# Relative attention's DRAM scratch cut from 64 heads to 16, each place written and read four times

## The chip, the cores and the metric

The kernel runs on one core of one Trainium2 chip. The metric is the device time of that core, from the launch of the program to its end, in microseconds (us). One execution was also taken by the hardware profiler; its rows are what the prediction is made from.

## What is computed

The input x has 4 sequences of 512 positions and 128 features. The program first adds a relative attention of 16 heads with 8 features each, and then six layers of windowed attention and a gated feed-forward. The change touches the first part alone. Cut to what matters:

```
x = x + attn(layernorm(x))          # the part that is changed
x = x + ffn(layernorm(x))           # six layers of local attention and feed-forward

# attn: B = 4 sequences, S = 512, H = 16 heads, P = 8 features of a head
pos = sinusoid_pos_emb(S, D) @ Wp + bp
content_score = einsum('bhsp,bhtp->bhst', q + u, k)
pos_score     = einsum('bhsp,htp->bhst', q + v, pos)
pos_score     = relative_shift(pos_score)
weights = softmax((content_score + pos_score) / sqrt(P))
out = einsum('bhst,bhtp->bhsp', weights, val)   # then @ Wo + bo

def relative_shift(x):              # per head: pad one column, reread with rows one shorter
    x = pad(x, one zero column on the left)     # [S, S + 1]
    return x.reshape(S + 1, S)[1:, :]           # [S, S]
```

All data is float32. There are 4 x 16 = 64 heads, each with a 512 x 512 matrix of position scores.

## The kernel before

The relative shift needs a row to be reread under another row length, which the kernel does through DRAM. The position scores of a head are written to `scratch_w` as 512 rows of 513 values (one zero column ahead), and read back as 512 rows of 512 values from one row further on. `scratch_w` has 64 heads, so each is written once and read once, at a place of its own.

The work goes in 128 rounds `r` (`ROUNDS`). A round handles a pair of heads and one of the four steps `i` of 128 rows; two rounds make one transfer `n = r // 2`, so a pair of heads takes two transfers (`n // 2` is the number of the pair), and there are 64 writes and 64 reads. Each queue and engine runs its own program in order:

- TensorE makes the position scores of round r (L905, `ps_b<-posm,qvT`), and 20 rounds behind (`LAG`) the content scores of round c = r - 20 (L905, `ps_b<-kTm,quT`), the transposes of round c - 1 (L931), and the sums with the values (L950).
- ScalarE (ACT) copies the position scores of round r to `wrows` (L1004), a ring of `NW` = 4 transfers. Before it fills a slot again it waits until the write that used it has landed (`written`). 12 rounds behind (`READ_AT`) it issues the read of transfer n into `shifted` (L1013), a ring of `NR` = 6, after a wait for the two writes of that pair and for VectorE to have taken the slot's last contents. It also does the exponentials (L1020).
- The SyncE queue (SP) issues the write of transfer n (L896) once the four copies of it are done (`w_copied`). It has nothing else to do in this stage.
- VectorE (L967) waits at round c for the read of transfer c // 2 (`read`), adds it to the content scores and takes the row's extreme into `lowest`; GpSimd (POOL, L991) scales the result `less`.

A write takes two heads' 128 partitions with two steps' rows each, 1026 KB in packets of 4104 bytes; a read is 1024 KB in packets of 4096 bytes. All transfers of the stage run on the same 16 DMA engines. The stage ends with a barrier of all engines before the output projection (L1037 and on), and the six layers follow.

Of the kernel before, what the change touches and what calls it, by code (L numbers as in the profile page):

```python
# [5 lines left out]
F32, BF16, I32 = mybir.dt.float32, mybir.dt.bfloat16, mybir.dt.int32  # L6
# [4 lines left out]
BATCH, SEQ = 4, 512  # L11
# [5 lines left out]
H0, DP = 16, 8  # L17
# [21 lines left out]
def at_least(eng, sem, count):  # L39

    if count > 0:
        eng.wait_ge(sem, count)
# [682 lines left out]
def relative_attention(nc, x, w, scratch):  # L725
# [7 lines left out]
    with ExitStack() as ctx:  # L733
# [3 lines left out]
        def sem(name):  # L737
            return ctx.enter_context(nc.semaphore("a_" + name))

        S = SEQ  # L740
        STEPS = S // P
# [12 lines left out]
        with ExitStack() as first:  # L754
# [16 lines left out]
            with nc.Block() as block:  # L771
                @block.sync
                def _(sp):
                    for dst, src in ((ident[:, :], w["ident"]), (wpT[:, :], w["wpT"][:, :, 0, :].rearrange("h p d -> (h p) d")),
                                     (table[:, :], w["fcols"][:, 1, 0:S]), (wproj[:, :, :], w["wproj"]),
                                     (cols[:, :], w["cols"]), (rows[:, :, :], w["rows"])):
                        sp.dma_start(dst, src).then_inc(s["loaded"], 16)
# [77 lines left out]
        with ExitStack() as second:  # L855
            def sb2(name, shape):
                return second.enter_context(nc.sbuf_tensor(name, shape, F32))
# [5 lines left out]
            ROUNDS = UNITS * STEPS * 2  # L863
            LAG, READ_AT = 20, 12
            NW, NR = 4, 6
            wrows = sb2("wrows", [P, NW, 2, 2, S + 1])
            shifted = sb2("shifted", [P, NR, 2, 2, S])
            less = sb2("less", [P, 2, 2, S])
# [9 lines left out]
            read = [sem(f"read{n}") for n in range(NR)]  # L878
            flat = scratch.rearrange("n s c -> n (s c)")

            def of(r):

                return r // (2 * STEPS), r % STEPS, r // STEPS % 2 * 2

            def in_slot(slots, n):
                return 16 * (n // len(slots) + 1)

            with nc.Block() as block:
                @block.sync
                def _(sp):  # L890

                    for n in range(ROUNDS // 2):
                        u, i, g = of(2 * n)
                        sp.wait_ge(s["w_copied"], 4 * n + 4)
                        rows_of = scratch[4 * u + g:4 * u + g + 2, :, :].rearrange("h (p i) c -> p h i c", i=STEPS)
                        sp.dma_start(rows_of[:, :, i:i + 2, :].rearrange("p h i c -> p h (i c)"),  # L896
                                     wrows[:, n % NW, :, :, :].rearrange("p h i c -> p h (i c)")).then_inc(written[n % NW], 16)

# [95 lines left out]
                @block.scalar  # L994
                def _(act):
                    act.wait_ge(s["zeroed"], 1)
                    for r in range(ROUNDS + LAG + 6):
                        c = r - LAG
                        if r < ROUNDS:
                            n = r // 2  # L1000
                            at_least(act, written[n % NW], 16 * (n // NW))
                            for k in range(2):
                                act.wait_ge(s["w_made"], 2 * r + k + 1)
                                nc.scalar.copy(wrows[:, n % NW, k, r % 2, 1:S + 1], ps[:, k, :]).then_inc(s["w_copied"], 1)  # L1004
                        n = (r - READ_AT) // 2
                        if r % 2 == 0 and 0 <= n < ROUNDS // 2:

                            u, i, g = of(2 * n)
                            for done in range(n // 2 * 2, n // 2 * 2 + 2):
                                act.wait_ge(written[done % NW], in_slot(written, done))  # L1010
                            at_least(act, s["c_taken"], 4 * (n - NR + 1))
                            src = flat[4 * u + g:4 * u + g + 2, S:(S + 1) * S].rearrange("h (p i t) -> p h i t", i=STEPS, t=S)
                            act.dma_start(shifted[:, n % NR, :, :, :].rearrange("p h i t -> p h (i t)"),  # L1013
                                          src[:, :, i:i + 2, :].rearrange("p h i t -> p h (i t)")).then_inc(read[n % NR], 16)
                        t = c - 1
                        if 0 <= t < ROUNDS:
                            at_least(act, s["o_summed"], t // 2 - 1)
                            for k in range(2):
                                act.wait_ge(s["p_turned"], 2 * t + k + 1)
                                nc.scalar.activation(pT[:, t // 2 % 2, t % 2 * 2 + k, :], ps[:, 4 + k, :], ACT.Exp  # L1020
                                                     ).then_inc(s["p_ready"], 1)
                        m = (c - 3) // 2
                        if c % 2 and 0 <= m < UNITS * STEPS and m % STEPS == STEPS - 1:
                            n = m // STEPS
                            act.wait_ge(s["o_summed"], m + 1)
                            at_least(act, s["o_turned"], n)
                            nc.scalar.copy(oT[:, :], ps[:, 6, :]).then_inc(s["o_copied"], 1)
# [36 lines left out]
def whole_kernel(nc, x_in, out, attention, layers):  # L1064
    with ExitStack() as ctx:
        x1 = ctx.enter_context(nc.sbuf_tensor("x1", [P, TILES, D], F32))
        x_loaded, added, stored = (ctx.enter_context(nc.semaphore(n)) for n in ("x_loaded", "x_added", "out_stored"))
        scratch = nc.dram_tensor("scratch_w", [BATCH * H0, SEQ, SEQ + 1], F32).ap()
        tiled = "(t p) d -> p t d"
        with nc.Block() as block:  # L1070
            @block.sync
            def _(sp):
                sp.dma_start(x1[:, :, :], x_in.rearrange("b s d -> (b s) d").rearrange(tiled, p=P)).then_inc(x_loaded, 16)
                sp.wait_ge(x_loaded, 16)
        relative_attention(nc, x1, attention, scratch)
        x = ctx.enter_context(nc.sbuf_tensor("x", [P, TILES, D], F32))
        layer_norm_tiles(nc, x1, x, "norm2")
        local_layers(nc, x, layers)
        with nc.Block() as block:
            @block.vector  # L1080
            def _(dve):
                nc.vector.tensor_tensor(x[:, :, :], x[:, :, :], x1[:, :, :], ALU.add).then_inc(added, 1)  # L1082

            @block.sync
            def _(sp):
                sp.wait_ge(added, 1)
                sp.dma_start(out.rearrange("b s d -> (b s) d").rearrange(tiled, p=P), x[:, :, :]).then_inc(stored, 16)
                sp.wait_ge(stored, 16)
# [88 lines left out]
```

## Time and profile before

| what | value |
|---|---|
| device time, median of 3 runs | 2430.02 us (2418.19 to 2435.28) |
| device time of the profiled execution | 2422.32 us |
| its span (first to last instruction) | 2420.5 us |
| TensorE busy / VectorE / ScalarE / GpSimd | 87% / 63% / 50% / 58% of the span |
| DMA, whole program | 260.54 MB, mean 108 GB/s |
| mean granted TensorE clock | 0.959 of full speed |

The span is one execution; what lies around it is 2422.32 - 2420.5 = 1.8 us. The busy shares are means over stages that differ: the relative attention fills about the first fifth of the span, the six layers the rest. In the rows, "SPq" and "ACTq" are DMA issues of those engines' queues, "to landing" is the time from the issue of a transfer to its last signal, and a DMA share of 1.00 means that on average all 16 DMA engines had a packet under way (it passes 1.00 where packets of the two queues overlap on one engine).

### The profile page before, as it was taken

To read this page: it belongs to the slowest core of one execution; us is meant where nothing else is said; L and a number is where in the kernel's file an instruction comes from. 1 tells how busy PE (TensorE), PEld (TensorE's weight loads), DVE (VectorE), ACT (ScalarE), POOL (GpSimd) and SP (SyncE) were. 2 spreads that over 40 slices of the span, in tenths; PEclk is the share of its full clock that TensorE was granted. 3 is DMA by queue.
4 is the path that set the end of the run, shared out by engine and by line. 5 is a ranking of instruction groups with operands and counts; after the bars stand their busy time and mean duration, and the time that the engine had idled before them with its cause. 6 is when DMAs were issued, how large, how long until landed. Compare 5 with 4: busy or idle time off the path is not lost. (4 is left out here: it accounts for less than half of the span.)

```text
span 2420.5 us, 84613 instructions
## 1 busy us (share of the span) xinstructions
PE 2096.9 (87%) x36003; PEld 1418.7 (59%) x36003; DVE 1529.2 (63%) x2264; ACT 1217.4 (50%) x1652; POOL 1395.7 (58%) x2272
## 2 busy tenths in 40 slices
PE   4687788893889899999999999898999999999996
PEld 2154445552666666666666666666666666666664
DVE  4043334443777677777777767777777777777773
ACT  2365556741445555544555445554455445555542
POOL 0043334444776676676666666666666666676770
PEclk9599989996999999999999999999999999999998
DMA  1799999942222322232222322223222242222221
GB/s 48 221 310 283 270 293 318 366 153 59 72 62 63 97 60 58 63 94 61 65 57 59 97 61 66 55 57 104 57 64 57 57 109 61 55 67 58 57 63 28
DMA packets 124948, 260.54 MB, mean 108 GB/s; under 512 B 29300, under 2 KB 40224, under 8 KB 123808
## 3 DMA queue, kind: packets, MB, share of 16 engines
q1 hardware_dynamic: 107168, 188.03, 29.0%
q10 hardware_dynamic: 17408, 67.11, 9.6%
q8 instruction: 287, 4.70, 0.9%
q14 instruction: 85, 0.70, 0.1%
HBM read 86.08 MB, written 68.29 MB: 64 GB/s over the span
## 5 line engine op out<-in xcount | busy, mean ns | idle before, releaser
L223 POOL TENSOR_TENSOR roped<-turned 128x512 f32<-128x512 f32 x384 | 480.4, 1273 | 386.4 <-PE ring L424 381.9
L414 PE MATMUL ring<-wqkv,xT 128*128 128x512 f32 x1152 | 573.0, 620 | 6.0 <-ACT squares L288 4.0
L568 DVE TENSOR_TENSOR turned<-ring,ropes 128x1024 f32<-128x1024 f32 x384 | 451.4, 1217 | 99.8 <-PE ring L414 97.8
L991 POOL TENSOR_SCALAR less<-less,lowest 128x512 f32<-128x512 f32 x256 | 174.4, 692 | 347.8 <-DVE lowest L967 347.8
L258 POOL TENSOR_TENSOR roped<-roped,rnorm 128x1024 f32<-128x1024 f32 x192 | 361.1, 1902 | 13.8
L967 DVE CUSTOM_DVE_ANT_0 less<-ps_b,shifted 128x512 f32<-128x512 f32 x256 | 166.7, 689 | 311.6 <-PE ps_b L905 190.7
L414 PEld LDWEIGHTS ring<-wqkv,xT 128*128 128x128 f32 x1152 | 198.7, 192 | 173.2 <-issue 153.9
L347 ACT COPY oT<-ring 128x1024 f32<-128x1024 f32 x96 | 97.2, 1012 | 364.8 <-PE ring L476 364.8
L577 DVE TENSOR_REDUCE ss<-squares 128x16 f32<-128x1024 f32 x192 | 232.9, 1213 | 37.5 <-ACT squares L288 37.5
L905 PE MATMUL ps_b<-posm,qvT 32*128 32x512 f32 x512 | 171.0, 744 | 95.6 <-ACT wrows L1004 72.1
L1004 ACT COPY wrows<-ps_b 128x512 f32<-128x512 f32 x256 | 137.5, 590 | 192.4 <-PE ps_b L905 118.0
L288 ACT ACTIVATE squares<-ring 128x1024 f32<-128x1024 f32 x192 | 197.2, 1027 | 60.1 <-DVE turned L568 59.6
L613 DVE TENSOR_TENSOR attended<-ring,rinv 128x1024 f32<-128x1024 f32 x96 | 117.6, 1225 | 170.0 <-PE ring L466 170.0
L485 PEld LDWEIGHTS yps<-wo,oT 128*128 128x128 f32 x1536 | 187.9, 193 | 47.1 <-issue 45.6
L424 PE MATMUL ring<-ident_l,roped 128*128 128x128 f32 x1536 | 193.5, 277 | 15.0 <-POOL roped L258 14.7
L466 PEld LDWEIGHTS ring<-vwin,pT 64*32 64x32 f32 x12288 | 129.6, 105 | 120.1 <-ACT pT L340 60.2
L424 PEld LDWEIGHTS ring<-ident_l,roped 128*128 128x128 f32 x1536 | 175.3, 143 | 32.1 <-POOL roped L258 19.1
L485 PE MATMUL yps<-wo,oT 128*128 128x128 f32 x1536 | 188.9, 276 | 2.0 <-ACT oT L347 1.1
L466 PE MATMUL ring<-vwin,pT 64*32 64x64 f32 x12288 | 148.6, 226 | 44.0 <-issue 27.6
L334 ACT ACTIVATE probs<-probs 128x1024 f32<-128x1024 f32 x96 | 101.6, 1059 | 156.1 <-DVE probs L591 156.1
L931 PEld LDWEIGHTS ps_b<-ident_a,less 128*128 128x128 f32 x1024 | 115.9, 146 | 101.5 <-POOL less L991 63.0
L441 PEld LDWEIGHTS ring<-kT,qT 64*32 64x32 f32 x12288 | 138.6, 105 | 60.2 <-issue 57.3
(122 smaller groups left out, 3383.4 us busy)
## 6 DMA issues: line engine op xcount, KB each, us to landing
vwin<-v SPq DMA_DIRECT2D x1536, 64.0 KB, 2.3
scratch_w<-wrows SPq DMA_DIRECT2D x64, 1026.0 KB, 21.7
shifted<-scratch_w ACTq DMA_DIRECT2D x64, 1024.0 KB, 20.6
wqkv<-in_l_wqkv SPq DMA_DIRECT2D x6, 1536.0 KB
wo<-in_l_wo SPq DMA_DIRECT2D x24, 128.0 KB
w<-in_l_w SPq DMA_DIRECT2D x6, 342.0 KB
w<-in_l_w SPq DMA_DIRECT2D x6, 171.0 KB
out_dram<-x SPq DMA_DIRECT2D x1, 1024.0 KB, 5.1
```

The lines of the kernel that those rows point to most:

```text
L223: nc.gpsimd.tensor_tensor(halves[2][:, :, side, :], halves[0][:, :, side, :], halves[1][:, :, 1 - side, :], ALU.add).then_inc(s[name + "_a ...
L258: nc.gpsimd.tensor_tensor(whole, whole, norm, ALU.mult).then_inc(s[name + "_roped"], 1)
L288: nc.scalar.activation(squares[:, n, :], ring[:, room(name.upper()), :, :].rearrange("p b c -> p (b c)"), ACT.Square).then_inc(s[name + "_ ...
L414: last = nc.tensor.matmul(out[:, half, :], xT[:, t % SEQT * P:(t % SEQT + 1) * P], wqkv[:, layer_of(t), at + half * 512:at + (half + 1) * ...
L424: last = nc.tensor.transpose(out[:, j * P:(j + 1) * P], roped[:, n, j * P:(j + 1) * P], ident[:, :])
L466: last = nc.tensor.matmul(out[W * win:W * win + W, r, j * DH:(j + 1) * DH], pT[rows, j, W * win:W * win + W], vwin[rows, p, win, j * DH:(j ...
L485: last = nc.tensor.matmul(out[:, 0:D], oT[:, j, :], wo[:, layer_of(t), j, :], start=j == 0, stop=j == PAIRS - 1)
L568: ins = nc.vector.tensor_tensor(turned[:, n, part, :].rearrange("p (h d) -> p h d", d=DH), heads, table, ALU.mult)
L577: nc.vector.tensor_reduce(ss[:, n * HEADS:(n + 1) * HEADS], squares[:, n, :].rearrange("p (h d) -> p h d", d=DH), AX.X, ALU.add).then_inc( ...
L905: nc.tensor.matmul(ps[:, bank + k, :], q[at, here:here + P], keys(at, u % VARS, b), start=True, stop=True).then_inc(signal, 1)
L967: nc.vector.tensor_tensor_reduce(less[:, c % 2, k, :], ps[:, 2 + k, :], shifted[:, c // 2 % NR, k, c % 2, :], -SCALE0, HIGHEST, ALU.add, A ...
L991: nc.gpsimd.tensor_scalar(less[:, c % 2, k, :], less[:, c % 2, k, :], -1.0, lowest[:, c % 2, k:k + 1], ALU.mult, ALU.add).then_inc(s["scal ...
```

## The change

`scratch_w` is declared with 16 heads instead of 64. The pair with number `n // 2` uses place `(n // 2) % 8` of it, for its two writes and its two reads. From transfer 16 on, SP waits before each write until both reads of the pair that had the place before, transfers `(n // 2 - 8) * 2` and the next one, have landed. Nothing else differs: the instructions of every engine and their order are the same, the sizes and shapes of the transfers too.

```diff
             NW, NR = 4, 6
+            KEPT = scratch.shape[0] // 2
...
+            def place(pair):
+                return pair % KEPT * 2
...
                     for n in range(ROUNDS // 2):
                         u, i, g = of(2 * n)
                         sp.wait_ge(s["w_copied"], 4 * n + 4)
-                        rows_of = scratch[4 * u + g:4 * u + g + 2, :, :].rearrange("h (p i) c -> p h i c", i=STEPS)
+                        if n // 2 >= KEPT:
+
+                            for done in range((n // 2 - KEPT) * 2, (n // 2 - KEPT) * 2 + 2):
+                                sp.wait_ge(read[done % NR], in_slot(read, done))
+                        rows_of = scratch[place(n // 2):place(n // 2) + 2, :, :].rearrange("h (p i) c -> p h i c", i=STEPS)
                         sp.dma_start(rows_of[:, :, i:i + 2, :].rearrange("p h i c -> p h (i c)"),
                                      wrows[:, n % NW, :, :, :].rearrange("p h i c -> p h (i c)")).then_inc(written[n % NW], 16)
...
-                            src = flat[4 * u + g:4 * u + g + 2, S:(S + 1) * S].rearrange("h (p i t) -> p h i t", i=STEPS, t=S)
+                            src = flat[place(n // 2):place(n // 2) + 2, S:(S + 1) * S].rearrange("h (p i t) -> p h i t", i=STEPS, t=S)
...
-        scratch = nc.dram_tensor("scratch_w", [BATCH * H0, SEQ, SEQ + 1], F32).ap()
+        scratch = nc.dram_tensor("scratch_w", [H0, SEQ, SEQ + 1], F32).ap()
```

## Rows read from the trace of the kernel before

**Rows 1.** Windows: busy us (count) by engine, granted clock, DMA share, GB/s.

```profile
54.70:115.90 61.20, 39.45 (x80) 9.53 (x80) 0.01 (x1) 19.46 (x38) 0.00 (x0) 0.50 0.68 208
115.90:180.00 64.10, 55.42 (x616) 33.03 (x616) 28.53 (x89) 41.43 (x80) 27.57 (x41) 0.94 1.08 311
180.00:400.00 220.00, 171.41 (x1892) 102.35 (x1892) 80.53 (x255) 127.08 (x243) 80.10 (x118) 0.92 1.05 287
...
410.00:490.00 80.00, 70.49 (x847) 42.80 (x848) 37.03 (x118) 56.45 (x109) 36.43 (x54) 1.00 1.03 365
490.00:545.60 55.60, 51.38 (x564) 31.12 (x560) 26.13 (x82) 21.92 (x41) 26.23 (x39) 1.00 0.39 125
545.60:2420.50 1874.90, 1678.10 (x31814) 1182.28 (x31812) 1327.40 (x1619) 930.97 (x1110) 1215.46 (x2008) 0.98 0.26 66
```

**Rows 2.** Waits from 200 to 400 us: total us, times, longest.

```profile
DVE less L967 <- PE ps_b L905: 65.6, 26, 4.9
ACT wrows L1004 <- DMA scratch_w<-wrows: 58.6, 21, 4.1
...
PEld ps_b L905 <- ACT wrows L1004: 49.6, 27, 3.5
```

**Rows 3.** Waits from 410 to 485 us.

```profile
ACT wrows L1004 <- DMA scratch_w<-wrows: 4.3, 3, 2.3
```

**Rows 4.** Transfers of scratch_w issued from 180 to 400 us.

```profile
L1013 ACTq DMA_DIRECT2D shifted<-scratch_w x30: 366/366/367, 180.9 to 397.9; - x30
L896 SPq DMA_DIRECT2D scratch_w<-wrows x29: 359/359/360, 185.2 to 394.8; - x29
...
DMA to landing us min/median/max: 19.6/25.3/30.0
```

**Rows 5.** Transfers of scratch_w issued from 410 to 490 us.

```profile
L896 SPq DMA_DIRECT2D scratch_w<-wrows x13: 359/360/363, 414.3 to 485.7; - x13
...
DMA to landing us min/median/max: 11.6/16.5/20.0
```

**Rows 6.** Transfer 16's write, the first that would reuse a place.

```profile
L896 SPq DMA_DIRECT2D scratch_w<-wrows x1: 360/360/360, 155.6 to 155.6; - x1
```

**Rows 7.** Transfer 1's read, the later of the two it would wait for.

```profile
L1013 ACTq DMA_DIRECT2D shifted<-scratch_w x1: 367/367/367, 96.2 to 96.2; - x1
...
DMA to landing us min/median/max: 9.4/9.4/9.4
```

**Rows 8.** The closest pair: write of transfer 62.

```profile
L896 SPq DMA_DIRECT2D scratch_w<-wrows x1: 363/363/363, 479.8 to 479.8; - x1
```

**Rows 9.** And the read of transfer 47, for which it would wait.

```profile
L1013 ACTq DMA_DIRECT2D shifted<-scratch_w x1: 367/367/367, 423.1 to 423.1; - x1
...
DMA to landing us min/median/max: 18.5/18.5/18.5
```

**Rows 10.** Timeline around an ACT read issue, which has three waits.

```profile
89.48 0.59 ACT L1004 COPY wrows<-ps_b 128x512 f32<-128x512 f32 x1 [2.21 <-PE ps_b L905]
89.59 0.39 ACTq L1013 DMA_DIRECT2D shifted<-scratch_w  x1
```

**Rows 11.** DMA issues of the page: size, median us to landing.

```profile
scratch_w<-wrows SPq DMA_DIRECT2D x64, 1026.0 KB, 21.7
shifted<-scratch_w ACTq DMA_DIRECT2D x64, 1024.0 KB, 20.6
```

**Rows 12.** Windows of 10 us each, columns as in rows 1.

```profile
80.00:90.00 10.00, 6.22 (x12) 1.50 (x12) 0.00 (x0) 3.36 (x8) 0.00 (x0) 0.50 0.45 180
90.00:100.00 10.00, 6.22 (x12) 1.50 (x12) 0.00 (x0) 3.36 (x8) 0.00 (x0) 0.50 1.03 234
100.00:110.00 10.00, 6.23 (x12) 1.50 (x12) 0.00 (x0) 3.36 (x7) 0.00 (x0) 0.50 1.02 228
110.00:120.00 10.00, 6.82 (x23) 2.20 (x24) 1.84 (x5) 2.95 (x7) 1.37 (x2) 0.50 1.00 359
240.00:250.00 10.00, 7.26 (x78) 4.27 (x80) 3.36 (x13) 5.12 (x10) 3.71 (x6) 0.83 1.10 245
...
280.00:290.00 10.00, 9.38 (x118) 5.83 (x116) 4.12 (x13) 6.47 (x13) 4.19 (x7) 0.96 1.06 325
```

## The prediction

> **What bounds the kernel now.** I read the windows first, since the change touches one stage. The reader should see in [rows 1] that the relative attention's exchange with DRAM runs from 54.7 to about 545.6 us, and that its bound changes on the way. From 180 to 400 us the DMA engines are full (share 1.05) and yet move only 287 GB/s, while no engine is busy for more than 171.4 of 220 us (TensorE) and its granted clock is down at 0.92. From 410 to 490 us they are as full (1.03) but move 365 GB/s, and TensorE is busy for 70.5 of 80 us at clock 1.00. The same transfers, so, are slow in one stretch and fast in another.
>
> The list of waits says the same from the engines' side. In the slow stretch ScalarE stands for 58.6 us, 21 times, before it may fill a slot of `wrows` whose write hasn't landed, and TensorE's weight loads for 49.6 us on ScalarE's copies [rows 2]. VectorE's largest wait (65.6 us) is for TensorE's scores, which is the same delay handed on: its own wait for a read hardly shows. In the fast stretch ScalarE's wait for writes is 4.3 us [rows 3]. Thus the chain in the slow stretch is write landing, copy, scores, next write; in the fast one it is the round's compute.
>
> The pace per transfer comes from the issues. 29 writes from 185.2 to 394.8 us are 28 steps, 209.6 / 28 = 7.49 us each [rows 4]; 13 writes from 414.3 to 485.7 us are 12 steps, 71.4 / 12 = 5.95 us each [rows 5]. One step moves a write and a read, 1026 + 1024 KB [rows 11], 2.10 MB. 2.10 MB in 7.49 us is 280 GB/s and in 5.95 us 353 GB/s, near what [rows 1] has for these stretches. What follows at 545.6 us, 1874.9 us of layers, comes after a barrier and isn't touched by the change, so each us won or lost here is one at the end.
>
> **Part 1, the new waits.** 48 writes (transfers 16 to 63) each get two waits on reads. The question is whether such a read can still be out. Transfer 16 is written at 155.6 us [rows 6]; it would wait for reads 0 and 1, and read 1 is issued at 96.2 us and lands 9.4 us later, at 105.6 [rows 7]. That leaves 50.0 us. I went through all 48 pairs by their issue times: the closest is write 62 at 479.8 us [rows 8] with read 47, issued at 423.1 us and landed at 441.6 [rows 9], 38.2 us ahead. Even with the longest landing of the slow stretch, 30.0 us [rows 4], it would be 56.7 - 30.0 = 26.7 us ahead. The code says that this is no luck of one execution: the copies of transfer n need TensorE's round 2n, and TensorE gets there only after the transposes of round 2n - 22, thus after VectorE has taken round 2n - 22, whose read (transfer n - 11) has then landed. The wait asks for transfers n - 16 and n - 15 at most. The wait can't be the last to be met whatever the rates are. Its stall is 0.
>
> What is left is the time of the instructions themselves on SP's sequencer. No row has SP with three waits. From below it is 0, and a gain is excluded, for a wait that is met takes no work away. From above, the nearest row is ScalarE's queue: a read's issue, which has two waits for writes and one for VectorE ahead of it, stands 0.11 us after the start of the copy before it [rows 10]. With 0.11 us on each of 48 writes and all of it on the path, that is 5.3 us. I take 0, because the write then meets a DMA queue that is full: it lands 19.6 us or more after its issue in the slow stretch [rows 4] and 11.6 us or more in the fast one [rows 5], so several transfers are in flight and the engines have other packets to work on. In the fast stretch ScalarE needs the landing only three steps later. If that cover were gone the 5.3 us would be the price. Queued behind the waiting instruction is SP's next write and nothing else, for SP has no other work in this stage; who waits for it would be ScalarE (slot of `wrows`, and its read's issue).
>
> **Part 2, the addresses.** This is what the change really changes: the number of bytes, packets and transfers stays, the order stays, the distance between a write and its read stays, but 64 heads' worth of DRAM becomes 16. What this does to the rate of a transfer no row shows, as every place is used once. So it is bounded from both sides over the 47 steps from write 16 (155.6 us, [rows 6]) to write 63 (485.7 us, [rows 5]), 330.1 us, or 7.02 us a step.
> - Gain at most: all 47 steps at the fast stretch's pace, which TensorE then sets: 47 x 5.95 = 279.7 us, 50.4 us less.
> - Loss: the slow stretch's pace for all, 47 x 7.49 = 352.0 us, 21.9 us more. Further out, the lowest rate with reads and writes side by side is 228 GB/s [rows 12], 2.10 / 0.228 = 9.2 us a step, 432 us, 102 us more.
>
> Which is nearest? The first 16 heads have been seen: while transfers 10 to 17 are written and 5 to 13 are read, the stretch of 115.9 to 180 us moves 311 GB/s at share 1.08 [rows 1], 6.75 us a step. And they show both a 228 and a 359 GB/s within 20 us [rows 12], as do the heads of the middle (245 and 325 within 40 us, [rows 12]). If the rate hung on the place alone, the 16 heads kept would run at 311 GB/s: 47 x 6.75 = 317 us, 13 us less than now. If it hangs on how the two queues' packets meet in time, nothing changes. Rates that swing this much within one place speak for the second; I take 0, and keep 13 us of gain as part of the range of this case.
>
> The same row of 287 GB/s at a full share [rows 1] can be held against a rule. The Trainium skill (DMA: Bandwidth & Descriptors, section Latency and other measured facts) reports that DMA copies with row pitches of large powers of two lose half of their rate or more, that a few KiB of padding restores it, and that this doesn't depend on how many tiles are touched; it calls the mechanism an inference. Here the head's pitch (513 x 512 x 4 bytes, 1 MiB and 2 KiB) and the row's pitch are the same before and after, and only the number of places falls, so by that rule the term is 0 too, where a reading of the rows by place gives 13 us less. No row here tests it.
>
> **Sum.** 2422.3 us (the profiled execution) + 0 (stall) + 0 (issue) + 0 (rate) = 2422.3 us. That execution is 7.7 us under the median of the three runs, 2430.0 us, which range over 17 us. The best guess of a new median is between the two: 2426 us. About 1% (24 us) is what a measurement of this kernel can tell from no change.
>
> **The rivals.**
> - *The smaller region is easier on DRAM.* The slow stretch goes away in part or in whole. For it: something slows the middle that doesn't slow heads 50 and on, and heads 0 to 15 are at the faster side (311 against 287 GB/s). Against it: the swings inside any group of heads. In whole it gives 2426 - 50 = 2376 us; half of it 2401 us. It counts as faster by over 1% from 24 us on, when the mean step falls below 7.02 - 24 / 47 = 6.51 us, 323 GB/s.
> - *Writes and reads now run over the same 16 heads and hinder each other (slower).* Before, each write went to a place never touched; now a write of place p comes while other places of the same 16 MB are read, and a write follows a read of the same bytes. For it: with writes alone the engines move 180 GB/s at a share of 0.45, and as soon as reads join, at 90 us, only 234 at 1.03 [rows 12], so the two kinds do disturb each other. Against it: they do that at distinct places already, and a read still follows its write by 6 transfers. It decides from 24 us on: a mean step above 7.53 us, below 279 GB/s. At the slow stretch's pace throughout it would be 2448 us, still within 1%; at 245 GB/s [rows 12], 8.6 us a step, 2426 + 73 = 2499 us; at 228, 2528 us.
> - *The new wait bites.* It needs a read that lands more than 56.7 us after its issue [rows 8, 9], against at most 30.0 [rows 4], and the code's order excludes it. Its cost would be a stall of the only write queue, but I see no case for it.
> - *The change doesn't do what it says*, for instance because places were already reused. In the code they weren't, with 64 heads and no modulus.
>
> **How the numbers follow.** No change beyond noise, with the small gain of 13 us and the 5.3 us loss inside: 0.60. The first rival by over 1%: 0.24, since there is a clear slow stretch to win back and the place is one of two explanations for it. The second by over 1%: 0.15. A wait or anything else that costs over 1%: 0.01. So faster 0.24, same 0.60, slower 0.16. The range that should hold 8 in 10 leaves out the first rival near its full size (below 2385 us, 0.09) and the second at its worst (above 2470 us, 0.09). The likeliest case's own range is 2405 to 2445 us: the runs' own 2418 to 2435, less 13 us and more some 10 us for a slow stretch that reaches further.
>
> **What the profile of the changed kernel would show.** If right: 64 writes and 64 reads of the same sizes; no wait of SP for reads, and SP's issues right behind the copies; a first stage that again ends near 545 us, with a slow stretch whose rate is 260 to 330 GB/s at a share over 1, ScalarE's wait for writes about 60 us in it and a granted clock of about 0.92. The slow stretch needn't lie at the same time. If the first rival is right, ScalarE's wait for writes falls to a few us, the clock stays at 1.00 from 120 us on, 360 GB/s hold to the end of the writes, and the stage ends near 495 us. If the second is right, the rate drops from transfer 16 on, at about 156 us, and not before. The prediction fails if the rate of a DRAM transfer depends on the region that it goes to by more than 8%.

## The result, and the profile after

The changed kernel takes 2416.23 us (median of 20 runs, 2408.74 to 2422.51), the kernel before 2426.68 us (median of 20 runs, 2416.53 to 2437.08). The ratio is 0.9956 with a 95% interval of 0.9943 to 0.997: 10.5 us less, within 1%, but clear of the noise. The forecast was 2426 us and no change. In the third group of experiments below, one of the nine executions of the kernel before took 7783.93 us, for a cause that isn't known, and no ratio uses it.

Windows of the changed kernel, columns as in [rows 1]:

```profile
54.70:115.90 61.20, 39.45 (x80) 9.54 (x80) 0.05 (x1) 19.49 (x37) 0.00 (x0) 0.50 0.68 215
115.90:180.00 64.10, 56.92 (x629) 33.65 (x630) 29.15 (x91) 43.95 (x85) 28.62 (x42) 0.94 1.06 314
180.00:400.00 220.00, 176.93 (x2016) 106.28 (x2015) 86.32 (x272) 134.08 (x259) 84.92 (x125) 0.95 1.04 307
410.00:480.00 70.00, 58.78 (x702) 35.68 (x704) 29.55 (x95) 46.02 (x89) 29.65 (x44) 0.98 1.06 315
...
538.60:2413.40 1874.80, 1676.69 (x31814) 1181.18 (x31812) 1327.03 (x1619) 930.47 (x1110) 1215.39 (x2008) 0.98 0.26 66
```

The reader should hold the last column against [rows 1]. The slow stretch got faster (307 against 287 GB/s) and the fast one got slower (315 against 365 GB/s); the first two rows are alike, and the layers take 1874.8 against 1874.9 us. What had been a slow middle and a fast end has, over stretches as long as these, become one rate (314, 307 and 315 GB/s). Over the 48 writes from transfer 16 on:

```profile
L904 SPq DMA_DIRECT2D scratch_w<-wrows x48: 359/359/369, 156.9 to 478.5; - x48
...
  ACT wrows L1012: 64.3, 26
```

That is 321.6 us for 47 steps, 6.84 us each, against 330.1 us and 7.02 us before ([rows 6] and [rows 5]): 8.5 us less. The profiled spans differ by 2420.5 - 2413.4 = 7.1 us, as write 16 was issued 1.3 us later (156.9 against 155.6 us). ScalarE's waits for a write between 200 and 400 us went from 58.6 [rows 2] to 51.7 us, and between 410 us and the end of the writes from 4.3 [rows 3] to 11.2 us:

```profile
ACT wrows L1012 <- DMA scratch_w<-wrows: 51.7, 20, 4.6
```
```profile
ACT wrows L1012 <- DMA scratch_w<-wrows: 11.2, 5, 2.8
```

And the new waits: the list of SP's own waits from 150 to 480 us has one row, with ScalarE's copies and no read in it.

```profile
SPq L904 <- ACT wrows L1012: 311.4, 49, 9.5
```

So the question is why 16 places take 6.84 us a step on average, where 64 take 7.49 and then 5.95. Within that average the pace still swings, and not with the place. Transfers 24 to 28, 40 to 44 and 56 to 60 write heads 8 to 11, and begin on the next pair, in three passes:

```profile
L904 SPq DMA_DIRECT2D scratch_w<-wrows x5: 359/360/360, 205.6 to 236.0; - x5
```
```profile
L904 SPq DMA_DIRECT2D scratch_w<-wrows x5: 359/359/360, 323.4 to 348.3; - x5
```
```profile
L904 SPq DMA_DIRECT2D scratch_w<-wrows x5: 359/360/360, 430.6 to 458.0; - x5
```

Four steps took 30.4, 24.9 and 27.4 us.

### The profile page after: what moved, and what is told of

It reads as the page before. It is cut to its first block and busy times, and to the rows that moved or that the text cites. A ratio compares the mean times of both kernels' runs of the same rounds, so it can differ in the third digit from the quotient of the medians.

```text
span 2413.4 us, 84661 instructions
## 1 busy us (share of the span) xinstructions
PE 2092.8 (87%) x36003; PEld 1416.0 (59%) x36003; DVE 1528.8 (63%) x2264; ACT 1216.8 (50%) x1652; POOL 1395.6 (58%) x2272
## 5 line engine op out<-in xcount | busy, mean ns | idle before, releaser
L583 DVE TENSOR_REDUCE smax<-ring 128x16 f32<-128x1024 f32 x96 | 117.5, 1224 | 89.5 <-PE ring L441 89.0
```

## The experiments

They come in three groups, each on one chip, with the kernel before run beside them. The kernel before took 2460.28, 2459.37 and 2426.03 us on these three chips, so each ratio is to its own group. All edits are to the changed kernel. "Offset" is how far into the scratch tensor a head begins, less the whole MiB; head h of the packed scratch begins at h x (1 MiB + 2 KiB), so its offset is 2 KiB x h.

### First group: is it the waits, the number of bytes, or the place?

**The waits alone.**

```diff
-            KEPT = scratch.shape[0] // 2
+            KEPT = 8
...
-                return pair % KEPT * 2
+                return pair * 2
...
-        scratch = nc.dram_tensor("scratch_w", [H0, SEQ, SEQ + 1], F32).ap()
+        scratch = nc.dram_tensor("scratch_w", [BATCH * H0, SEQ, SEQ + 1], F32).ap()
```

> Scratch of 64 heads with a place of its own for each, as before, but with the change's two waits on reads ahead of each write from transfer 16 on. Theory A (the gain of 10 us is in the addresses, fewer bytes of DRAM are touched): no gain, ratio 1.000 within 0.002. Theory B (the waits shift SP's issues a little and space the two queues' packets better): ratio about 0.996. If the waits cost anything by themselves it would be up to 5.3 us, ratio 1.002.

Measured: 2459.26 us, ratio 0.9997 (0.9979 to 1.0015). The 96 added waits neither cost nor give anything that can be measured; of the two parts of the change, the addresses are left for the gain.

**The last 16 heads of 64** (`KEPT = 8`, 64 heads declared):

```diff
-                return pair % KEPT * 2
+                return 48 + pair % KEPT * 2
```

> Scratch declared with 64 heads, but only heads 48 to 63 of it are used, each pair's place four times, with the change's waits. Theory A1 (fewer distinct bytes, whichever they are): ratio 0.996, like the change. Theory A2 (the first 16 heads are a faster place, by 311 against 287 GB/s): no gain here, unless the last heads are fast too; then, since the stretch at 365 GB/s was at heads 50 to 63, up to 50 us less, ratio 0.98. Theory A3 (a smaller tensor moves the other DRAM tensors): ratio 1.000, as the declared size is that of before.

Measured: 2374.18 us, ratio 0.9657 (0.9633 to 0.9681): 86 us less than before, eight times the change's own gain, by another choice of 16 places. In its trace the same view as above reads:

```profile
L904 SPq DMA_DIRECT2D scratch_w<-wrows x48: 359/360/369, 157.2 to 437.4; - x48
...
  ACT wrows L1012: 4.4, 3
```

280.2 us for 47 steps, 5.96 us each, and ScalarE stands for writes for 4.4 us where it was 64.3. That is the pace of the compute. From 180 to 400 us the window has the DMA engines as full as ever and yet at 353 GB/s, with the granted clock at 1.00:

```profile
180.00:400.00 220.00, 198.04 (x2405) 119.97 (x2404) 102.31 (x323) 157.71 (x305) 100.82 (x148) 1.00 1.05 353
```

**16 places spread over 64 heads** (`KEPT = 8`, 64 heads declared):

```diff
-                return pair % KEPT * 2
+                return pair % KEPT * 8
```

> 16 heads' places used four times each, but 8 heads apart, so that they span the whole 64 heads of scratch. Theory A1a (the number of distinct bytes counts): ratio 0.996. Theory A1b (the span of addresses counts): ratio 1.000.

Measured: 2451.3 us, ratio 0.997 (0.9951 to 0.999). The number is the one expected if the count of distinct bytes matters, and the interval leaves out the 1.000 of a span of addresses; but the last and the middle 16 (next group) write as many bytes and are far from it, so the count isn't the cause. These 16 places sample the whole range of offsets, 0 to 114 KiB, in the same order three times after transfer 16, and the trace shows the order. The issues of transfers 24 to 28, 40 to 44 and 56 to 60 (heads 32, 33, 40 and 41, the slowest four steps of each pass):

```profile
L904 SPq DMA_DIRECT2D scratch_w<-wrows x5: 359/359/360, 208.5 to 243.5; - x5
```
```profile
L904 SPq DMA_DIRECT2D scratch_w<-wrows x5: 359/360/360, 330.8 to 365.6; - x5
```
```profile
L904 SPq DMA_DIRECT2D scratch_w<-wrows x5: 359/360/360, 451.8 to 486.7; - x5
```

And those of transfers 16 to 20, 32 to 36 and 48 to 52 (heads 0, 1, 8 and 9, the fastest of each pass):

```profile
L904 SPq DMA_DIRECT2D scratch_w<-wrows x5: 359/359/360, 155.5 to 180.4; - x5
```
```profile
L904 SPq DMA_DIRECT2D scratch_w<-wrows x5: 359/359/360, 273.2 to 300.1; - x5
```
```profile
L904 SPq DMA_DIRECT2D scratch_w<-wrows x5: 359/359/360, 394.3 to 421.8; - x5
```

Four steps take 35.0, 34.8 and 34.9 us there, and 24.9, 26.9 and 27.5 us here. What is under way at an issue began some four steps earlier (landings take 19.9 to 31.5 us in these stretches), so the pattern can't be put down to single heads, but it comes back with the places, within one execution, and so isn't one of time or of chip.

**12 heads.**

```diff
-        scratch = nc.dram_tensor("scratch_w", [H0, SEQ, SEQ + 1], F32).ap()
+        scratch = nc.dram_tensor("scratch_w", [12, SEQ, SEQ + 1], F32).ap()
```

> 12 heads instead of 16 (each pair's place by every sixth pair; the reads waited for are those of transfers n - 12 and n - 11, which have landed by the code's order). Theory A1 (fewer bytes, faster): at least the change's gain, ratio 0.993 to 0.996. Theory that the gain comes from one region or from one distance between written and read places: it may go either way, 0.99 to 1.01. If the wait begins to bite, SP would stand for reads, and the ratio would pass 1.00.

Measured: 2438.03 us, ratio 0.9924 (0.9895 to 0.9954). It fits "fewer bytes are faster" as well as "the lowest offsets are a little better", so it decides nothing alone.

### Second group: which part of the address?

**The first 16 of 64 declared** (`KEPT = 8`, 64 heads declared, places as in the change):

> The change with the scratch still declared with 64 heads, of which the first 16 are used. The last 16 of 64 gave a ratio of 0.966 and a write every 5.95 us throughout. Theory P (the place inside the scratch sets the rate): the same as the change, about 0.996, since the places are the same. Theory T (a declared size of 64 heads puts the tensor, or its neighbours, where it is fast when only 16 heads are used): about 0.97.

Measured: 2450.75 us, ratio 0.9967 (0.9952 to 0.9983), the change's own ratio within both intervals. The declared size has no effect that shows. Its 47 steps take 351.2 us, 7.47 us each:

```profile
L904 SPq DMA_DIRECT2D scratch_w<-wrows x48: 359/360/362, 157.6 to 508.8; - x48
```

**The middle 16 of 64** (as above, with `24 + pair % KEPT * 2`):

> Heads 24 to 39 of a scratch of 64, each pair's place used four times. Theory P: this is the slow stretch of before (7.5 to 8.4 us a write), so all of the stage from transfer 16 on runs at some 7.8 us a write: 47 x 7.8 = 367 us against 330 us, ratio about 1.015. Theory U (reuse of places is what makes it fast, the last 16 being an accident of order): ratio under 1.00.

Measured: 2486.54 us, ratio 1.0111 (1.0077 to 1.0145).

```profile
L904 SPq DMA_DIRECT2D scratch_w<-wrows x48: 359/360/362, 164.3 to 555.4; - x48
...
  ACT wrows L1012: 130.3, 39
```

391.1 us for 47 steps, 8.32 us each. Reuse of 16 places is slower than no reuse, if they are the wrong 16. The row of 180 to 400 us has 252 GB/s at share 1.01; TensorE is busy for 160.1 us, against 198.0 with the last 16, and its granted clock is 0.88 against 1.00:

```profile
180.00:400.00 220.00, 160.14 (x1672) 95.47 (x1665) 71.45 (x226) 111.95 (x214) 70.14 (x103) 0.88 1.01 252
```

**16 heads, begun 96 KiB into the tensor.**

```diff
-        scratch = nc.dram_tensor("scratch_w", [H0, SEQ, SEQ + 1], F32).ap()
+        ahead, kept = 96 * 1024 // 4, H0 * SEQ * (SEQ + 1)
+        whole = nc.dram_tensor("scratch_w", [ahead + kept], F32).ap()
+        scratch = whole[ahead:ahead + kept].rearrange("(n s c) -> n s c", s=SEQ, c=SEQ + 1)
```

> 16 heads that begin 96 KiB into the scratch tensor. Head h starts at h x (1 MiB + 2 KiB), so heads 48 to 63 start 48 MiB + 96 KiB in. Theory L (the low part of the offset, 2 KiB for each head, sets how the channels are met): fast like the last 16, ratio about 0.97. Theory H (the high part, the region of DRAM): like the change, 0.996.

Measured: 2381.71 us, ratio 0.9686 (0.966 to 0.9711). 96 KiB of unused DRAM ahead of the heads are worth 69 us over the same 16 heads without it (2450.75 us in this group). Its writes from transfer 16 on, 282.8 us for 47 steps, 6.02 us each:

```profile
L904 SPq DMA_DIRECT2D scratch_w<-wrows x48: 359/360/362, 156.5 to 439.4; - x48
...
  ACT wrows L1012: 6.6, 3
...
DMA to landing us min/median/max: 5.8/18.2/23.0
```

And its window of 180 to 400 us, to hold against that of the middle 16 (252 GB/s) on the same chip:

```profile
180.00:400.00 220.00, 196.83 (x2383) 118.92 (x2382) 100.41 (x317) 155.22 (x300) 99.46 (x146) 0.99 1.05 346
```

**The same, begun 48 MiB in** (`ahead = 48 * 1024 * 1024 // 4`):

> 16 heads that begin exactly 48 MiB into the scratch tensor, without the 96 KiB. Theory H: fast, ratio about 0.97. Theory L: like the change, 0.996.

Measured: 2448.9 us, ratio 0.9959 (0.994 to 0.9978), as if begun at 0, and 349.9 us for the 47 steps:

```profile
L904 SPq DMA_DIRECT2D scratch_w<-wrows x48: 359/360/370, 157.7 to 507.6; - x48
```

Heads 48 to 63 were fast for their 96 KiB, and not for their 48 MiB. This run and the one before it differ in the one number `ahead`.

### Third group: without reuse, and how far the rule goes

**64 places of their own, all at a good offset.** Four regions of 16 heads, 17 MiB apart, each begun at 96 KiB; no place is used twice and there are no waits on reads:

```diff
-            KEPT = scratch.shape[0] // 2
+            KEPT = 32
...
-                return pair % KEPT * 2
+                return pair % 8 * 2
...
-                        rows_of = scratch[place(n // 2):place(n // 2) + 2, :, :].rearrange("h (p i) c -> p h i c", i=STEPS)
+                        rows_of = scratch[n // 16][place(n // 2):place(n // 2) + 2, :, :].rearrange("h (p i) c -> p h i c", i=STEPS)
...
-        scratch = nc.dram_tensor("scratch_w", [H0, SEQ, SEQ + 1], F32).ap()
+        region, kept = 17 * 1024 * 1024 // 4, H0 * SEQ * (SEQ + 1)
+        whole = nc.dram_tensor("scratch_w", [4 * region], F32).ap()
+        scratch = [whole[n * region + k * 256:n * region + k * 256 + kept].rearrange("(n s c) -> n s c", s=SEQ, c=SEQ + 1)
+                   for n, k in enumerate((96, 96, 96, 96))]
```

The reads go to the same places.

> All 64 heads have a place of their own, no place is used twice and SP has no new wait, but the places lie in four regions of 16 heads whose first starts 96 KiB past a multiple of 1 MiB (region n begins at n x 17 MiB + 96 KiB). Theory L (the part of a place's offset below 1 MiB sets the rate): as fast as the 16 heads that begin at 96 KiB, ratio about 0.968, a write every 5.95 us. Theory U (it needs both the offset and the reuse of a small region): between 0.98 and 1.00.

Measured: 2370.68 us against 2426.03, ratio 0.9775 (0.9749 to 0.9802). The expected 0.968 was worked out on chips where the kernel before took 2460 us. In us it is where the other fast ones are (2374.18 and 2381.71), and the trace has the compute's pace, with no wait of ScalarE for a write at all in the stretch (it would stand under "who waited for it"):

```profile
L904 SPq DMA_DIRECT2D scratch_w<-wrows x48: 359/360/363, 154.5 to 433.8; - x48
...
who waited for it (us, times):
busy tenths in 40 slices 0000000000000000000000000000000000000000
DMA to landing us min/median/max: 6.4/11.1/14.2
```

279.3 us for 47 steps, 5.94 us each. So reuse isn't needed for the fast pace.

**64 heads in one row from 96 KiB on** (`ahead` as above, `kept` for 64 heads):

> 64 heads with a place of their own in one row, beginning 96 KiB in, so that the low part of the offset runs from 96 KiB to 222 KiB in steps of 2 KiB. Theory L with a period of 128 KiB: transfers 0 to 15 fast, then the curve of before from its start, slow at heads 36 to 60, ratio 0.98 to 1.00. Theory L with a longer period or a single bad band at 40 to 90 KiB: fast to the end, ratio 0.968.

Measured: 2436.15 us, ratio 1.0045 (1.0025 to 1.0065). The expected curve came, with a worse total than was expected: fast while heads 12 to 25 are written (offset 120 to 146 KiB), slow for heads 30 to 60 (156 to 216 KiB). The writes of the two stretches:

```profile
L904 SPq DMA_DIRECT2D scratch_w<-wrows x14: 359/360/360, 132.1 to 209.3; - x14
```
```profile
L904 SPq DMA_DIRECT2D scratch_w<-wrows x31: 359/360/360, 246.1 to 480.4; - x31
```

77.2 / 13 = 5.94 us a step, and 234.3 / 30 = 7.81 us. A slow band about 128 KiB above the first one is there.

**Far offsets.** The four regions with `(352, 304, 608, 560)` for `(96, 96, 96, 96)`:

> As the four regions, but they begin 352, 304, 608 and 560 KiB past a multiple of 17 MiB, that is 256 or 512 KiB plus 96 or plus 48. Period of 128 or 256 KiB: transfers 16 to 31 and 48 to 63 slow (about 8.3 us a write), the others at 5.95 us; total between the change and the fast ones, ratio about 0.99. A single band below 128 KiB: all fast, 0.968. No rule of the low offset: some other pattern.

Measured: 2374.61 us, ratio 0.9783 (0.9765 to 0.9801), all of it fast, transfers 16 to 31 and 48 to 63 too:

```profile
L904 SPq DMA_DIRECT2D scratch_w<-wrows x48: 359/360/363, 155.0 to 434.3; - x48
```

So a period of 128 KiB doesn't hold beyond the second band, at least not in regions 17 MiB apart.

**Reads from elsewhere.** `KEPT = 8`, 64 heads declared; `other` is a tensor of the layers' weights, so this kernel leaves the relative shift's data out and its time alone is of use:

```diff
-                return pair % KEPT * 2
+                return (24 if pair < 16 else 48) + pair % KEPT * 2
...
-            flat = scratch.rearrange("n s c -> n (s c)")
+            flat = other.rearrange("l d e -> (l d e)")[0:2 * S * (S + 1)].rearrange("(n x) -> n x", n=2)
...
-                            src = flat[place(n // 2):place(n // 2) + 2, S:(S + 1) * S].rearrange("h (p i t) -> p h i t", i=STEPS, t=S)
+                            src = flat[0:2, S:(S + 1) * S].rearrange("h (p i t) -> p h i t", i=STEPS, t=S)
```

> Leaves the relative shift's data out: the reads of shifted come from one fixed 2.1 MB of the layers' weights, while the writes go to heads 24 to 39 (offset 48 to 78 KiB, slow) in transfers 0 to 31 and to heads 48 to 63 (fast) in 32 to 63. If the slow place hinders the writes: about 8 us a write in the first half and 6 in the second. If it hinders the reads, or needs reads and writes at the same place: one pace in both halves.

One execution, 2411.19 us. Writes of transfers 16 to 31, and of 34 to 63:

```profile
L904 SPq DMA_DIRECT2D scratch_w<-wrows x16: 359/360/360, 154.5 to 268.8; - x16
...
DMA to landing us min/median/max: 24.6/27.0/30.4
```
```profile
L904 SPq DMA_DIRECT2D scratch_w<-wrows x30: 359/360/370, 290.6 to 469.9; - x30
...
DMA to landing us min/median/max: 13.7/19.7/24.5
```

114.3 / 15 = 7.62 us a step, then 179.3 / 29 = 6.18 us, near the compute's pace, with the reads at one and the same place in both halves. Windows with both queues' rate, the first with heads 24 to 39 written (and the first issues to heads 48 and on), the last with heads 48 to 63:

```profile
180.00:290.00 110.00, 82.78 (x922) 48.90 (x923) 39.04 (x122) 62.89 (x120) 38.25 (x56) 0.94 1.05 277
...
300.00:460.00 160.00, 141.48 (x1728) 85.32 (x1728) 72.45 (x229) 110.64 (x214) 71.04 (x104) 1.00 1.05 350
```

This one execution speaks for the place that is written being enough to make the stage slow. Whether reading from such a place costs too, it doesn't tell; and the two halves come in one order only, though the middle 16 show no such trend in time (252 GB/s from 180 to 400 us, 263 from 400 to 480), and in the 16 spread places slow and fast steps alternate.

## Why the prediction was right, and where it wasn't

**The waits (part 1): right.** Stall 0 and issue 0 were predicted; the waits alone gave 0.9997, and SP's list has no read in it. The interval's upper end, 1.0015, is 3.7 us of 2460, below the bound of 5.3 us.

**The rate (part 2): the time was in the range, the value taken was the wrong one of two.** The prediction had both explanations before it: the rate hangs on the place, 13 us less, or on how the packets meet in time, 0. It took 0, since "rates that swing this much within one place speak for the second". This step failed. Measured were 10.5 us less in 20 runs and 8.5 us less over the 47 steps in the profile, and the experiments show that the place was the explanation: 252 GB/s at the middle 16 heads and 346 at 16 heads begun 96 KiB in, on one chip, where the prediction named a difference of over 8% by region as the sign of its failing. That "no change within 1%" came true all the same owes something to luck: the change keeps heads 0 to 15, whose rate is near the old mean, while the middle 16 took 27 us more and the last 16 took 86 us less than the kernel before on their chips.

The first 16 heads' 6.75 us a step, read from the rate of the stretch of 115.9 to 180 us, came near the 6.84 us measured (the chip of the second group, where every kernel with slow places took longer, had 7.47 us for them). Part of that is luck too. The stretch has the writes of transfers 10 to 19, not 10 to 17, and by their issues, as the two other stretches were read, a step is 55.8 / 9 = 6.20 us:

```profile
L896 SPq DMA_DIRECT2D scratch_w<-wrows x10: 359/360/360, 120.6 to 176.4; - x10
```

The swings were real, within one place as well (30.4, 24.9 and 27.4 us for the same four steps of the changed kernel), but they lie on top of a place's mean and told nothing about it; the two means over longer stretches, 287 and 365 GB/s at the same share, were the evidence, and they belonged to different places. What makes the swings isn't known.

**Why so little came of it.** The change gives up a slow band and a fast one together. Of the old 47 steps, heads 20 to 48 took 7.49 us and heads 51 and up 5.95 us [rows 4, 5]; heads 0 to 15, which stand in for both, are between them at 6.84 us. That 16 is fewer than 64 isn't needed to explain it.

**The first rival** (a smaller region is easier on DRAM) named 2376 us, which is what good places give and the change didn't. Its mechanism isn't borne out: 64 places of their own at good offsets take 2370.68 us, and 16 at bad ones 2486.54 us beside 2459.37. (12 heads came out lower than 16, 0.9924 against 0.9967, on different chips and with intervals that meet; whether that is their number or their offsets, no run tells.) **The second rival** (writes and reads in one region hinder each other) falls with the last 16 heads, which are reused as closely and run at the compute's pace. Its limit of 7.53 us a step was for a kernel of 2426 us and can't be held against the 8.32 us of the middle 16, which were measured beside one of 2459.37.

**The rule on pitches.** The Trainium skill (DMA: Bandwidth & Descriptors, section Latency and other measured facts) has large power-of-two row pitches as slow (half of the rate lost at 4 and 8 MiB, less at 2 MiB) whatever the number of tiles touched. That the number doesn't matter agrees with 64 places being as fast as 16 (2370.68 us against 2374.18), though both run at the compute's pace, where a small difference in rate wouldn't show. But at one and the same pitch the rate here runs from 252 to 346 GB/s on one chip by the start alone, which the rule doesn't speak of; and whether its supposed cause, aliasing of channels, is at work here, no run tested.

**What stays open.** Which address bits make a place slow. Slow were offsets of about 40 to 90 KiB and 156 to 216 KiB, middling 0 to 30, fast 96 to 146; regions at 304, 352, 560 and 608 KiB were fast, so that no plain period of 128 KiB fits, and their 17 MiB spacing was changed along with the offset. The offset isn't all, either: with the heads begun at 96 KiB, a landing took 18.2 us in the median with 16 reused places and 11.1 us in the four regions, on another chip. The tensor's own start in DRAM isn't known. So it is also open what differs between the chips, the memory or where the tensor lies in it: the kernel before took 2426 to 2460 us on them, the fast places 2371 to 2382, so the gain over the kernel before (55 to 86 us) varies and the fast time hardly does. And not all packets of a slow place are slow: from 180 to 400 us the median packet took 160 ns with the middle 16 and with the last 16 alike, but 14 to 16% of the middle 16's took over 400 ns, and about 5% of the last 16's. Which these are isn't known.

**The better version.** The change plus 96 KiB ahead of the heads took 2381.71 us beside 2459.37, and the four regions without reuse 2370.68 us beside 2426.03. Both beat the kernel before on their chips by more than the change does (10.5 us); the first keeps the small scratch. Little more is to be had from the place, as they run at 6.02 and 5.94 us a step, near the 5.95 us of a stretch in which ScalarE hardly waits for writes.

## What to carry to other kernels

Where DMA engines are full but their GB/s differ between two stretches that issue the same transfers, set the rate beside the place in DRAM that each stretch uses, over windows long enough to even out the swings of single ones; a place is cheap to move. When a change of buffer count gives a small gain, test it once with the same count at other addresses, before the count is believed. And a wait can be priced at nothing without a trace if the program's order already implies it several steps earlier.

## What the hardware showed that I hadn't expected

The start of a DRAM buffer, moved by 96 KiB, moved the 47 steps from 351.2 to 282.8 us, 7.47 to 6.02 us each, and the kernel by 69 us (2450.75 to 2381.71 us); the declared size differs between these two as well, but against the start at 48 MiB, where it is only the start, it is 67 us (2448.9 us). With the DMA share at 1.01 to 1.05, transfers of the same size and shape ran at 252 GB/s (the middle 16) to 353 (the last 16): a full DMA share says that packets are under way, not that they move at full speed. The slow places showed in ScalarE's waits for landings (130.3 us with the middle 16, 4.4 with the last 16) and in the time to landing of the same stretches, 28.1 against 17.1 us in the median, the middle 16 first:

```profile
DMA to landing us min/median/max: 5.8/28.1/35.6
```
```profile
DMA to landing us min/median/max: 6.0/17.1/22.6
```
